# Reading a block's first further column in place, and loading the next only where there is one

## The reference

```python
# x: 6250 x 512; src, dst: 100000 edges, sorted by dst
def gnn(x, edge_index, W1, b1, W2, b2):
    src, dst = edge_index
    agg = jax.ops.segment_sum(x[src], dst, num_segments=6250)
    h = jax.nn.relu((x + agg) @ W1 + b1)
    return jax.nn.relu(h @ W2 + b2)

x = x + gnn(layernorm(x), (src, dst), W1, b1, W2, b2)
x = x + lstm(layernorm(x)[None], W_f, b_f, W_i, b_i, W_c, b_c, W_o, b_o)[0]
```

## Time and profile before

| what | value |
|---|---|
| median of three runs | 2840.35 us (2840.02 to 2848.08) |
| profiled execution | 2835.44 us, span 2833.9 us, mean granted clock 0.972 |
| PE busy | 2506.7 us, 88% of the span |
| DVE busy | 2090.2 us, 74% |
| ACT busy | 1585.3 us, 56% |
| POOL busy | 1019.9 us, 36% |
| graph part | from the first gather at 203.8 us to about 1398 us |

### The profile page before, as it was taken

The page is one execution under the profiler, slowest core; times in us unless marked ns, Lnnn a source line. Parts: engine busy times, 40 slices in busy tenths (PEclk is TensorE's granted clock), DMA queues, the critical chain, the costliest instruction groups (busy, mean ns, idle before and its releaser), DMA issues.

```text
span 2833.9 us, 45183 instructions
## 1 busy us (share of the span) xinstructions
PE 2506.7 (88%) x10574; PEld 1840.8 (65%) x10575; DVE 2090.2 (74%) x5442; ACT 1585.3 (56%) x3682; POOL 1019.9 (36%) x1022
## 2 busy tenths in 40 slices
PE   6977999999999999998799988888887888788776
PEld 5765787788888778786566656666664555555444
DVE  5847888888888888887578766666666667666665
ACT  4644544454554444453267744444445888777775
POOL 0307777777777777776300000000000000033332
PEclk9998999999999999999899999999998999999998
DMA  8548988888898888887566557777776777689996
GB/s 238 154 137 249 281 265 259 250 272 271 269 280 270 253 254 265 249 265 227 171 166 185 147 168 237 235 234 231 236 237 170 212 204 213 187 233 260 270 266 188
DMA packets 209753, 648.73 MB, mean 229 GB/s; under 512 B 48762, under 2 KB 76794, under 8 KB 179954
## 3 DMA queue, kind: packets, MB, share of 16 engines
q1 hardware_dynamic: 136888, 410.93, 49.9%
q0 software_dynamic: 72816, 237.24, 28.3%
HBM read 493.87 MB, written 154.16 MB: 229 GB/s over the span
## 4 chain that ended last, share of the span: by engine, by line
PE 29%; DMA 6%; ACT 6%; DVE 6%; issue 2%; SPq 1%; DVEq 0%; ACTq 0%
PE acc L1506 24%; DMA xg<-total_rows 6%; PE hturn L1524 3%; ACT acc L1444 3%; ACT tc L1436 2%; ACT gate L1410 1%; DVE ic L1779 1%; PE acc L1532 1%; DVE total L1750 1%; DVE h L1792 1%; DVE c L1784 1%; DVE fc L1772 1%; DVE total L1752 1%; PE acc L1535 0%; DVE state L1766 0%
## 5 line engine op out<-in xcount | busy, mean ns | idle before, releaser
L1506 PE MATMUL acc<-W_high,state 128*125 128x512 f32 x2224 | 629.4, 417 | 71.6 <-ACT acc L1444 69.7
L1506 PEld LDWEIGHTS acc<-W_high,state 128*125 128x125 f32 x2224 | 410.4, 192 | 206.5 <-ACT acc L1444 88.2
L1359 POOL TENSOR_TENSOR out<-h,lx 125x512 f32<-125x512 f32 x50 | 64.3, 1286 | 1224.2 <-DVE h L1792 1224.2
L809 POOL DMA_INDIRECT rows<-ln_table,slab x400 | 400.7, 1002 | 249.5 <-issue 145.3
L809 POOL DMA_INDIRECT Wh<-ln_table,slab x400 | 430.4, 1076 | 121.9 <-issue 119.8
L910 PE MATMUL agg<-high,onehot 128*125 128x512 f32 x800 | 332.8, 416 | 29.7 <-DVE onehot L1007 18.5
L1506 PE MATMUL acc<-W_high,hT 128*125 128x512 f32 x784 | 325.1, 415 | 8.3 <-issue 0.2
L1020 DVE TENSOR_TENSOR low_part<-rows,high 128x512 fp32r<-128x512 f32 x400 | 254.1, 691 | 98.1 <-ACT high L866 83.5
L910 PE MATMUL agg<-low_part,onehot 128*125 128x512 f32 x800 | 322.0, 403 | 0.0
L1506 PE MATMUL acc<-W_low,hT 128*125 128x512 f32 x784 | 308.6, 394 | 0.0
L1772 DVE TENSOR_TENSOR fc<-gate,c 125x256 f32<-125x256 f32 x376 | 162.9, 433 | 188.6 <-ACT gate L1410 179.3
(11 more groups left out here) (211 smaller groups left out, 4483.1 us busy)
## 6 DMA issues: line engine op xcount, KB each, us to landing
xg<-total_rows SPq DMA_DIRECT2D x100, 896.0 KB
xg<-gate_rows SPq DMA_DIRECT2D x88, 896.0 KB
gate_rows<-gout SPq DMA_DIRECT2D x100, 448.0 KB
total_rows<-total SPq DMA_DIRECT2D x50, 896.0 KB
hT<-h_steps SPq DMA_DIRECT2D x98, 250.0 KB, 3.7
lx<-x_rows POOLq DMA_DIRECT2D x50, 250.0 KB, 8.6
out_dram<-out POOLq DMA_DIRECT2D x50, 250.0 KB, 8.7
h_steps<-hT SPq DMA_DIRECT2D x49, 250.0 KB, 3.2
```

Source lines behind the costliest of these rows:

```text
L809: e.indirect_dma_start(out=rows[j // 2][:, j % 2 * D:(j % 2 + 1) * D], out_offset=None, in_=table[:, :], in_offset=bass.IndirectOffsetOnAx ...
L1506: m = e.matmul(acc[n][0:L, :], stationary[:, k, :], weights[:, k, n // 2, n % 2].rearrange("p s c -> p (s c)"), start=begins, stop=(k == K ...
```

## The change

The copy into `pair_x` and its semaphore are gone: the gather and the one-hot read `slab_x[par]`. The first further column of a block is visited without any load. The load of a column's pairs now stands ahead of the visit of that same column and is done for the second and later ones only, inside an `If` of its own. The wait behind the last load is gone with that load. Since the gather now reads `slab_x` itself, SP waits, before it loads `slab_x` for a block, until PE has used all further columns of the blocks up to the one two before. It reads how many those are as index 3 of `ranges`, which DVE fills with index 0 of the block before.

```diff
@@ block_ranges (table part, DVE)
                 after_own(e.memset(ranges[:, :, 3:4], 0))
+                after_own(e.tensor_copy(ranges[:, 1:BLOCKS, 3], ranges[:, 0:BLOCKS - 1, 0]))
@@ load_slab (graph part, SP)
-                begin, = range_of(e, b, 2, 3)
+                begin, visited = range_of(e, b, 2, 4)
...
                 if free is not None:
                     hold(e, s_passed, s_beyond, free - 1)
+                    hold(e, s_passed, s_visit_x, visited + 1)
@@ one (graph part, POOL)
-                def beyond(n, g):
+                def visit(n):
                     hold(e, s_passed, s_visit_x, n + 1)
-                    hold(e, s_passed, s_slab_x, 16)
-                    e.tensor_copy(pair_x[:, :], slab_x[par][:, :]).then_inc(s_pair_x, 1)
-                    hold(e, s_passed, s_pair_x, n + 1)
                     e.inc_swdge_sem([s_rows_x], [16], mode="sub")
                     e.indirect_dma_start(
                         out=rows_x[:, :], out_offset=None, in_=table[:, :],
-                        in_offset=bass.IndirectOffsetOnAxis(ap=pair_x[:, 0:1], axis=0),
+                        in_offset=bass.IndirectOffsetOnAxis(ap=slab_x[par][:, 0:1], axis=0),
                     ).then_inc(s_rows_x, 16)
-                    e.tensor_scalar(onehot_x[:, :], node_id[:, :], pair_x[:, 1:2].bitcast(F32), None,
+                    e.tensor_scalar(onehot_x[:, :], node_id[:, :], slab_x[par][:, 1:2].bitcast(F32), None,
                                     ALU.is_equal).then_inc(s_hot_x, 1)
+                    hold(e, s_passed, s_hot_x, n + 2)
+
+                def load_and_visit(n, g):
+                    hold(e, s_passed, s_visit_x, n + 1)
                     e.inc_swdge_sem([s_slab_x], [16], mode="sub")
-                    at_g = nc.s_assert_within(begin + (g + (COLUMNS + 1)) * P, 0, E + SPARE - P,
+                    at_g = nc.s_assert_within(begin + (g + COLUMNS) * P, 0, E + SPARE - P,
                                               skip_runtime_bounds_check_because=BOUNDED)
                     e.dma_start(slab_x[par][:, :], edges[bass.ds(at_g, P)]).then_inc(s_slab_x, 16)
-                    hold(e, s_passed, s_hot_x, n + 2)
-
-                def first_slab():
-                    hold(e, s_passed, s_own, b * OWN + CLEARED)
-
-                def last_slab():
-                    hold(e, s_passed, s_slab_x, 16)
+                    hold(e, s_passed, s_slab_x, 16)
+                    visit(n)
 
                 hold(e, s_passed, s_slab_first[par], times * 16 + 16)
-                columns_beyond(e, before, extra, beyond, first_slab, last_slab)
+                extra = nc.s_assert_within(extra, 0, MOST, skip_runtime_bounds_check_because=BOUNDED)
+                with e.If(extra > 0):
+                    hold(e, s_passed, s_own, b * OWN + CLEARED)
+                    visit(before)
+                    with e.If(extra > 1):
+                        with e.Fori(1, extra) as g:
+                            load_and_visit(before + g, g)
                 e.sem_inc(s_beyond, 1)
```

More of the change, by code:

```diff
@@ L629, in graph_part @@
         slab_x = [sb(ctx, f"slab_x{n}", [P, 2], I32) for n in range(2)]
-        pair_x = sb(ctx, "pair_x", [P, 2], I32)
         rows_x = sb(ctx, "rows_x", [P, D])
@@ L662, in graph_part @@
         s_rows_x = sem(ctx, "s_rows_x")
-        s_pair_x = sem(ctx, "s_pair_x")
         s_slab_first = [sem(ctx, f"s_slab_first{n}") for n in range(2)]
@@ L733, in range_of, with columns_beyond @@
             return values
-        def columns_beyond(e, before, extra, visit, begin_with=None, end_with=None):
+        def columns_beyond(e, before, extra, visit):
             extra = nc.s_assert_within(extra, 0, MOST, skip_runtime_bounds_check_because=BOUNDED)
             with e.If(extra > 0):
-                if begin_with is not None:
-                    begin_with()
                 with e.Fori(0, extra) as g:
                     visit(before + g, g)
-                if end_with is not None:
-                    end_with()
         @block.sync
@@ L828, in beyond @@
                         out=rows_x[:, :], out_offset=None, in_=table[:, :],
-                        in_offset=bass.IndirectOffsetOnAxis(ap=pair_x[:, 0:1], axis=0),
+                        in_offset=bass.IndirectOffsetOnAxis(ap=slab_x[par][:, 0:1], axis=0),
                     ).then_inc(s_rows_x, 16)
-                    e.tensor_scalar(onehot_x[:, :], node_id[:, :], pair_x[:, 1:2].bitcast(F32), None,
+                    e.tensor_scalar(onehot_x[:, :], node_id[:, :], slab_x[par][:, 1:2].bitcast(F32), None,
                                     ALU.is_equal).then_inc(s_hot_x, 1)
+                    hold(e, s_passed, s_hot_x, n + 2)
+                def load_and_visit(n, g):
+                    hold(e, s_passed, s_visit_x, n + 1)
                     e.inc_swdge_sem([s_slab_x], [16], mode="sub")
-                    at_g = nc.s_assert_within(begin + (g + (COLUMNS + 1)) * P, 0, E + SPARE - P,
+                    at_g = nc.s_assert_within(begin + (g + COLUMNS) * P, 0, E + SPARE - P,
                                               skip_runtime_bounds_check_because=BOUNDED)
                     e.dma_start(slab_x[par][:, :], edges[bass.ds(at_g, P)]).then_inc(s_slab_x, 16)
-                    hold(e, s_passed, s_hot_x, n + 2)
-                def first_slab():
+                    hold(e, s_passed, s_slab_x, 16)
+                    visit(n)
+                hold(e, s_passed, s_slab_first[par], times * 16 + 16)
+                extra = nc.s_assert_within(extra, 0, MOST, skip_runtime_bounds_check_because=BOUNDED)
+                with e.If(extra > 0):
                     hold(e, s_passed, s_own, b * OWN + CLEARED)
-                def last_slab():
-                    hold(e, s_passed, s_slab_x, 16)
-                hold(e, s_passed, s_slab_first[par], times * 16 + 16)
-                columns_beyond(e, before, extra, beyond, first_slab, last_slab)
+                    visit(before)
+                    with e.If(extra > 1):
+                        with e.Fori(1, extra) as g:
+                            load_and_visit(before + g, g)
                 e.sem_inc(s_beyond, 1)
```

## The result

The changed kernel takes 2823.86 us (median of 8 runs, 2816.69 to 2830.49), the kernel before in the same comparison 2841.59 (8 runs, 2838.65 to 2848.08). The ratio is 0.9935, 95% interval 0.9917 to 0.9953: 18 us faster, where 28 were forecast. The time is inside the range of 2802 to 2829 and 12 us above the likeliest value.

What follows compares the result with a forecast made beforehand. TensorE was taken as the bound, waiting on late gathers in the graph part. Terms -28.6 + 0.2 + up to 0.5 gave -28 us: 2807 from the profiled 2835.4, 2812 off the median 2840.35; range 2802 to 2829.

Steps and rivals of the forecast that it cites:

- The bound and the mechanism: Graph part: TensorE bounds; further columns make POOL's gathers late, so TensorE waits; 36.6 us of long stages in all.
- The stretch of 4.5 us: POOL, last gather of a block with a further column to the next block's first: 4.5 us (3.5 to 5.8) for 9.0.
- two readings of the landing: POOL behind the one-hot: 1.4 to 2.3 us idle left if landing counts from issue's end, 0.63 more if from its start.
- The step that failed: Graph part, plain blocks: POOL gains over a microsecond per block, so five stages lose about 1.6 us each; 8 us stay.
- The leads to start from: POOL's lead over TensorE behind the seven further columns: old lead plus TensorE's stage, less 16 gathers, less 4.5; 12.6 to 16.1 us.
- The clipped gain: Graph part: gathers' landing sets the stalls, each column keeps two long stages; 22 us stay, 14 go, 2826 us; 15%.
- the likeliest case: Graph part: 8 of 36.6 us of long stages stay, 28.6 go; 2812 us, own range 2806 to 2823; 75%.
- The wait under another name: POOL behind a further column would still wait for its buffer, DVE's low part; time stays about 2840 us; 6%.
- The slower case: POOL, all 50 blocks: leaving the new branch nest costs unhidden time; 2842 us at 2 us per block, 2863 at 2.5; 4%.
- The signs named ahead: Graph part: 4.5 us without copy or load, hin waits under 1 us, no stage over 25, no 0.88 clock, end 28 earlier.
- three signs of being wrong: Graph part: idle behind the one-hot above 3 us, 0.30 between plain blocks growing, or stages losing time at leads above 15.
- What was added: SP's second register load 0 to 0.5 us, its added wait met with 5 to spare; DVE's one-row instruction 0.2 us.

Runs made afterwards that it cites:

- narrow low part: Changed kernel, DVE taking the low part of only 64 of each 512 gathered values after block 0; 0.9820 of the kernel before.
- late ranges: Changed kernel with GpSimd reading the block's three values of ranges behind its 16 gathers instead of ahead; 0.9917 of the kernel before.
- the kernel with everything: Changed kernel with three orders changed on DVE and ScalarE, one-hot ahead of its gather, register loads behind the 16 gathers; 0.9877 of the kernel before.

## Why the prediction was right or wrong

*The bound and the mechanism: right.* Further columns delay POOL, the lead over TensorE falls, TensorE waits. Without them 2.0 us of long stages are left, and the load put back takes the gain back.

*The stretch of 4.5 us: too short by 0.9.* The idle time ahead of the gather is 0.30 and not 0.6, the lower end. The idle time behind the one-hot was taken at 2.2 and is 2.6 to 3.0 in six of the blocks, inside the bounds up to 3.0, and 5.54 behind block 41; without that block the mean stretch is 4.95. Of the prediction's two readings of the landing the second was right: the profile counts it from the start of the issue (2.02 us for the load issued at 423.08), which leaves 4.34 - (2.02 - 0.63) = 2.95 in the first case. About 1.2 us of it are register loads.

*The step that failed: "POOL wins a microsecond and more on TensorE per plain block, so a lead of 13 is above 15.2 one stage later".* In the profile after, the leads from stage 10 on are 13.4, 13.95, 15.2 and 16.7: it takes two or three stages. So each column costs two or three stages instead of one, 0.3 to 2.8 us each, and 24.7 us stayed where the sum had 8. The sum took a block of POOL's as about 20.9 us. Over the nine blocks that come within two behind a further column (10, 11, 14, 15, 35, 36, 42, 43 and 48), start to start, it was 21.43 in the kernel before and is 22.09 in the changed one. Against a plain stage of 22.18 that wins 0.1 us; what brought the lead back was mostly TensorE's own long stages. With the narrow low part the same blocks take 20.91, a lead comes back by over a microsecond per block, and 2.4 us stay; how much of that is the higher lead at the start is open, as said there. That gathers can be held was visible in the kernel before: for eight blocks, four from 670 us on at a lead of 16.17 and four from 847 us on at 17.96, POOL's block took TensorE's 22.16 us without waiting between blocks, though 16 undisturbed gathers take 20.0.

*The leads to start from: 2 us too high.* Forecast behind the seven columns were 16.1, 14.9, 16.1, 13.3, 13.3, 12.6 and 12.7. Measured are 13.4, 12.0, 14.1, 11.7, 11.7, 11.7 and 10.2, 2.0 lower in the mean. Of this 0.9 is the stretch and 0.8 the 16 gathers of the column's own block, 21.84 us in the mean where they were 21.04; the sum kept them as they were. The sum itself slips twice: for block 13 it gives 17.53 + 23.00 - 21.42 - 4.5 = 14.6, and for block 47 it gives 12.6 + 23.00 - 19.9 - 4.5 = 11.2.

*The rivals.* The clipped gain (22 us stay, 14 go, 2826 us) came nearer than the likeliest case: 24.7 stayed, and the time is 2824. It had its cause in the landing times; without further columns these cost 2.0 us, so it came near by luck, and what kept the 24.7 is the low leads and their slow return. The wait under another name is refuted by the load put back. The slower case is refuted: 25 of the 42 plain blocks are still followed by the next within 0.35 us (33 before), and 14 of the other 17 are put down by the profile to the slab's load or to a buffer, all at leads of 15.2 us and more. With the load back its landing took 2.1 to 4.1 us, median 3.5. The nearly constant 2.0 us of the Trainium skill (DMA: Bandwidth & Descriptors, the chain of events of a DMA) is the low end of that, and the measurement decides.

*The signs named ahead.* Met: no copy and no load in the stretch, 0.30 us between plain blocks, no clock of 0.88 (from block 9 on the lowest is 0.93, in the stage at 1165.13, behind a wait of 2 us for hin). Missed: one wait for hin is over 1 us, two stages are over 25 us (25.28 and 25.53), and the last turn is 12 us earlier, not 28. Of the three signs of being wrong two came true in part: behind block 41 the idle stretch is above 3 us, and stage 41 lost 2.2 us at a lead of 16.5. The second was in the trace before already: the stages at 1146.34 and 1263.81 lost 4.21 and 4.02 us at leads of 16.7 and 16.2, so "behind the first stages none above it has" was a misreading. These two lost their time at their end, where TensorE waits for hin behind the next block's first gather, so it is the next block's lead that counts for them.

*What was added: right in the sum, wrong in two terms.* DVE's copy on one row took 1.02 us, not 0.2:

```profile
101.19 1.02 DVE L517 COPY ranges<-ranges 1x49 int32<-1x49 int32 x1
```

No cost of it shows: the first turn of hin came 1.1 us earlier than before, and over all executions it came at 231.4 to 235.9 us with this copy and at 233.3 and 234.8 without. The load of SP's registers, bound by nothing and 0.5, went from a median of 1.80 to one of 2.44 us. The added wait on SP showed no cost: TensorE used block 9's further column at 432.91, 0.8 us earlier than in the earlier trace rows, and nothing of SP stands in TensorE's waits.

## What to carry to other kernels

When one engine runs ahead of another, what a delay costs is decided by how far ahead it is and how fast the lead comes back, not only by how long the delay is. Take that speed block by block behind a delay, not from a mean. A wait is worth asking twice about where an engine stands behind its own last instruction: the load that nobody read cost more in its landing than in its issue. And when a wait vanishes by a new order, look where it stands now before counting it as won.

## What had not been expected of the hardware

- An indirect gather's issue on GpSimd took 0.95 us alone, and of those beside one of VectorE's low parts (128 x 512, two inputs) 22 in 100 took over 1.2 us, of those beside a one-hot (128 x 500, two inputs) 31 in 100, mostly up to 1.5. Cutting the low parts to 64 of 512 values took the mean of 800 gathers from 1.042 to 0.994 us.
- Behind block 41 the stretch was 2.3 to 3.0 us longer than the mean of the other six in all nine executions that had a further column and no load: 7.92 and 7.60 in the changed kernel, 6.54 with late ranges, 5.99 in the kernel with everything. It is always the same block, and it is neither a wait nor a register load: in all nine the gather starts 3.2 us behind the last wait, where it is at most 1.0 at the other six. What it is stays open. With the load back, as in the kernel before, it is 0.8 there too.
- A copy of 49 integers within one row took 1.02 to 1.06 us in all eleven executions that had it, where conversions and subtractions of 50 on the same row took 0.20 to 0.24.
